# A small matmul on zeros in front of each two experts' first layers, in a ViT tower with recurrent mixing and a mixture of experts

## What is computed

```
h = patches @ W.T + b                                   # 784 tokens of 64 numbers a step
h = h + rnn(layernorm(h))                               # h_t = tanh(x_t W_ih + h_(t-1) W_hh + biases)
h = h + ffn(layernorm(h))

def ffn(x):                                             # 16 experts, 2 chosen for each token
    gate_logits = x @ gate_w + gate_b
    topk_vals, topk_idx = top_k(gate_logits, 2)
    topk_w = softmax(topk_vals)
    h = relu(einsum('bsh,ehf->bsef', x, w1) + b1)       # first layer, 64 -> 128, for all 16 experts
    expert_out = einsum('bsef,efh->bseh', h, w2) + b2   # second layer, 128 -> 64
    y = x + sum over the chosen of topk_w * expert_out
    return layernorm(y) * gamma + beta
```

## Time and profile before

| | |
|---|---|
| median of 3 runs | 514.97 us (513.32, 514.97, 515.25) |
| the profiled execution | 513.06 us, span on the core 511.0 us |
| PE busy | 493.3 us (97% of the span), 2980 matmul records |
| DVE busy | 447.3 us (88%) |
| ACT busy | 342.9 us (67%) |
| POOL busy | 183.2 us (36%) |
| mean granted clock of PE | 0.987 of full speed |

### The profile page before, as it was taken

One profiled execution on the slowest core, in us unless ns is written; L12 is line 12 of the kernel. 1 busy time (PEld: TensorE's weight loads), 2 busy tenths in 40 slices (PEclk: granted clock), 3 DMA queues, 4 the chain that ended last, 5 costly groups with the idle time before them and its releaser, 6 DMA issues.

```text
span 511.0 us, 8780 instructions
## 1 busy us (share of the span) xinstructions
PE 493.3 (97%) x2980; PEld 324.1 (63%) x2980; DVE 447.3 (88%) x881; ACT 342.9 (67%) x586; POOL 183.2 (36%) x137
## 2 busy tenths in 40 slices
PE   8789999999999999999999999999999999999993
PEld 5465666666666666666766666666666666666652
DVE  1678888989989898998989999898989899999775
ACT  1556675868677695857668586767858676665652
POOL 3220304436152443616144262515335362223133
PEclk9989999999999999999999999999999999999997
DMA  6229193957639192775819395483919366481911
GB/s 145 75 67 226 35 221 82 199 126 167 162 80 228 49 223 79 160 168 113 196 36 221 96 195 130 104 205 84 232 38 216 94 135 159 117 196 47 227 40 31
DMA packets 31067, 69.04 MB, mean 135 GB/s; under 512 B 6720, under 2 KB 10800, under 8 KB 30896
## 3 DMA queue, kind: packets, MB, share of 16 engines
q1 hardware_dynamic: 31024, 68.49, 57.9%
HBM read 60.39 MB, written 8.08 MB: 134 GB/s over the span
## 4 chain that ended last, share of the span: by engine, by line
PE 90%; DVE 2%; issue 2%; DMA 1%; ACT 1%; SPq 1%; POOL 1%; POOLq 0%; DVEq 0%; ACTq 0%
PE pZ L911 38%; PE pO L928 35%; PE pA L863 3%; PE pA L830 2%; PE pA L853 2%; PE pA L880 2%; PE pA L942 2%; DMA gbias<-gate_b 1%; PE pB L892 1%; PE pA L843 1%; PE pB L942 1%; PE pB L880 1%; PE pA L854 1%; DVE prod L679 1%; PE pO L802 0%
## 5 line engine op out<-in xcount | busy, mean ns | idle before, releaser
L503 ACT ACTIVATE hexp<-pZ,b1c 128x784 f32<-128x784 f32 x256 | 221.5, 912 | 108.9 <-PE pZ L911 108.9
L928 PE MATMUL pO<-hexp,w2s 128*64 128x392 f32 x1024 | 198.5, 503 | 0.6 <-ACT hexp L503 0.3
L911 PE MATMUL pZ<-xt,w1hi 128*128 128x392 f32 x512 | 187.8, 367 | 1.4 <-ACT xt L431 1.4
L679 DVE SCALAR_TENSOR_TENSOR prod<-pO,b2c,spread 128x392 f32<-128x392 f32 x256 | 149.8, 620 | 31.8 <-PE pO L928 30.3
L911 PE MATMUL pZ<-xt,w1lo 128*128 128x392 f32 x512 | 173.8, 340 | 0.0
L911 PEld LDWEIGHTS pZ<-xt,w1hi 128*128 128x128 f32 x512 | 96.1, 188 | 46.9 <-issue 18.3
L366 POOL TENSOR_TENSOR inv_std<-var,nhalf 112x7 f32<-112x7 f32 x48 | 82.5, 1727 | 105.3 <-DVE var L569 105.3
L928 PEld LDWEIGHTS pO<-hexp,w2s 128*64 128x64 f32 x1024 | 70.2, 136 | 75.3 <-issue 62.2
L695 DVE TENSOR_TENSOR acc<-acc,prod 128x784 f32<-128x784 f32 x111 | 111.3, 1002 | 0.1
L911 PEld LDWEIGHTS pZ<-xt,w1lo 128*128 128x128 f32 x512 | 96.4, 188 | 0.0
L379 POOL TENSOR_TENSOR h2b<-h2c,bet 112x448 f32<-112x448 f32 x15 | 18.4, 1226 | 162.3 <-DMA h2c<-h_dram 162.3
(11 more groups left out here) (114 smaller groups left out, 503.3 us busy)
## 6 DMA issues: line engine op xcount, KB each, us to landing
spread<-gates_dram SPq DMA_DIRECT2D x126, 392.0 KB, 8.9
h_dram<-h SPq DMA_DIRECT2D x16, 248.1 KB, 2.4
h2c<-h_dram SPq DMA_DIRECT2D x16, 248.1 KB, 9.0
out<-yo SPq DMA_DIRECT2D x15, 196.0 KB, 9.1
xcur<-x_in SPq DMA_DIRECT2D x16, 112.0 KB, 7.8
xcur<-x_in SPq DMA_DIRECT2D x16, 84.0 KB, 8.9
w1f<-w SPq DMA_DIRECT2D x2, 512.0 KB, 5.8
spread<-gates_dram SPq DMA_DIRECT2D x4, 196.0 KB, 3.6
```

What stands on the lines that cost most here:

```text
L503: nc.scalar.activation(hexp[u % RING][:, :].rearrange("p (b c) -> p b c", b=2), halves(pZ[u % 2]), ACT.Relu, bias=b1c[:, u:u + 1]).then_in ...
L679: nc.vector.scalar_tensor_tensor(out=prod[q % RING][:, b * HALF:(b + 1) * HALF], in0=halves(pO)[:, b, :], scalar=b2c[:, q:q + 1], in1=spre ...
L911: last = nc.tensor.matmul(halves(pZ[e % 2])[:, b, :], w[:, e, :], xt[par][:, b * HALF:(b + 1) * HALF], start=(k == 0), stop=(k == 1))
L928: last = nc.tensor.matmul(halves(pO)[k * D:(k + 1) * D, b, :], w2s[:, e, :], hexp[e % RING][:, b * HALF:(b + 1) * HALF], start=True, stop= ...
```

## The change

In front of the first of two experts' first layers (even e), once PE has waited for what `pZ` needs, PE multiplies 32 columns of zeros by a 128 x 128 block of zeros into the first 32 columns of `pZ[0]`. The matmul with `w1hi` that follows starts a new sum there and writes over them. The very first expert (n = 0) has none, so there are 16 * 8 - 1 = 127 of these.

```diff
--- before.py
+++ after.py
@@ -906,6 +906,9 @@
                     pe.wait_ge(h1_kept, 2 * 2 + 2)
                 if not known(n, 2):
                     pe.wait_ge(h_ready, n - 1)
+                if e % 2 == 0 and not known(n, 1):
+
+                    nc.tensor.matmul(pZ[0][:, 0:32], busy[:, 0:128], busy[:, 0:32], start=True, stop=True)
                 for b in range(2):
                     for k, w in enumerate((w1hi, w1lo)):
                         last = nc.tensor.matmul(halves(pZ[e % 2])[:, b, :], w[:, e, :],
```

## The result

| | before | changed |
|---|---|---|
| median | 515.04 us (513.32 to 515.25, 4 executions) | 527.90 us (526.56 to 528.64, 4 executions) |
| the profiled execution | 513.06 us, span 511.0 | 527.29 us, span 525.2 |

The changed kernel is slower: the ratio is 1.0254, with a 95% interval from 1.0222 to 1.0287, so 13.1 us (11.4 to 14.8) at 515. The forecast was 527.5 us in a range from 524.3 to 532.4.

A forecast was written before the change was run, and what follows sets the result against it. The prediction took PE to be the bound, never held by another engine through some 460 us. 124 unhidden inserts x 0.108 us = 13.4 us, added to the mean of 514.15, gave 527.5 us, range 524.3 to 532.4.

The forecast's parts named there:

- PE is the only bound: In the loop from 38 to 500 us: PE is never held by another engine, its waits adding up to 1.2 us.
- The price is a second bare load: Behind each insert: the small matmul is too short to cover the load of `w1hi`, which costs 0.108 us.
- rows 10: Profile rows of lines 952 and 956: 14 loads of 112 with 64-column matmuls start in 1.37 us, 0.098 us each.
- low side: Lower bound, from line 880's transposes: 0.093 us for each of 121 inserts, 11.3 us, on the lowest execution: 524.3.
- Three inserts of the first step are hidden, up to three more later: Experts 2, 4 and 6, ahead of waits of 1.1 and 0.6 us, cost nothing; other short waits may swallow three more.
- The forecast's base: Whole kernel before the change: 514.15 us, the mean of four executions, to which 13.4 us was added.
- PE empties ahead of the insert since it needs the full array after tiles: Behind tiles: the emptying of about 0.08 us moves from `w1hi` to the insert, at no cost of its own.
- the first rival: Behind second layers: the insert's load is pulled ahead, 98 places cost nothing, 29 still 0.108 us: 517.3 us; 5%.
- the faster one: Behind tiles: the loads of insert and `w1hi` are both taken ahead, 98 places win 0.093 us each: 508.2 us; 4%.
- A second emptying: Between the small matmul and `w1hi`: PE empties again, some 0.08 us more for each insert, 537.5 us; 4%.
- hidden behind other engines' padding: Throughout PE's list: waits that the records don't show pad PE's busy time and the inserts fill those, 514 us; 2%.

## Why the prediction was right

**PE is the only bound.** Held. PE stays at 32.00 of 32.00 us, DVE and ACT lost share, and a step grew by 0.90 us, where the eight distances of 0.11 that were added in PEld come to 0.88.

**The price is a second bare load.** Held, by four independent edits: columns (232 cost next to nothing, 392 cost 0.178), place, number and width of weights. The forecast's 0.108 us was 0.004 too low; the step gives 0.112. Read to the nanosecond, the starts of the loads put the added distance at 0.109 us behind tiles and 0.112 behind the full-array transposes, 0.110 in the mean of the eight places; the other 2 ns stay open. The prediction's own rows 10 were nearest: 0.098 us for 112 columns of weights is 0.112 for 128. Its low side was not a price of loads: the 0.093 us of line 880's transposes (0.096 from load to load) goes with the columns that pass, 112 there and 128 at 0.109 us for line 942, though the former load 128 columns and the latter 112.

**Three inserts of the first step are hidden, up to three more later.** The waits shrank by 0.1 and 0.2 us as forecast. In the last part some five inserts' worth, 0.6 us, was swallowed rather than up to three. 13.4 us was forecast, and the inserts' share of the span's 14.2 us is 0.5 + 10.8 + 2.0 = 13.3 us: the price a little low and the swallowed part a little low cancel, which is luck. The remaining 0.9 us comes from the place of the low clock at the start. The forecast's base, 514.15 us, was likewise 0.9 us below the measured median of before, and its addition 0.3 us above the measured 13.1.

**PE empties ahead of the insert since it needs the full array after tiles.** The prediction gave this cause without rows that could separate it from the change of type. The run with half the array first spoke against it, and the two in plain f32 restored it, with the addition on f32r. The price of the insert doesn't hang on it.

**The rivals.** Behind tiles the load of zeros was not pulled ahead in any f32r run; the 0.61 us ahead of it stood. That settles the first rival and the faster one, which needed the same. It did go ahead once, in plain f32 with 64 columns, where shape and type were those of the second layers. So the pull-ahead that the Trainium skill describes ("TensorE: Matmul & The Clock Gate", section "Step-by-step: what each phase is for") is there, and a change of shape stops it. The Trainium skill, "TensorEngine Tiling (Array Packing)", section "Key Properties", says that switching the tiling mode needs a drain. The runs agree: from the last second-layer load to that of `w1hi` it takes 0.75 us (246.00 to 246.75 in the earlier trace rows), two passings of 0.33 and 0.09 of emptying. A second emptying (537.5 us) didn't occur, and nothing was hidden behind other engines' padding.

The Trainium skill's floor of about 25 ns for a small matmul ("TensorE: Matmul & The Clock Gate", section "Back-to-back issue gap"), taken as the price of an insert, would have given 3.1 us. The runs show four times that, because each matmul brings a load of its own width.

## What to carry to other kernels

In f32r and in plain f32, a matmul that was too short to cover a weight load cost that load: 0.11 us for 128 columns of weights, whether 32 or 232 columns pass, 0.08 for 96 behind tiles and 0.06 for 64. The transposes are another case: there the columns that pass set the distance. Read the price of a small matmul on a full PE from the distances between load starts, not from its record or its columns. Keep matmuls of one array shape together: each entry from 64 columns into the full array cost an emptying of some 0.09 us and a bare load of 0.11, and filler on the full array neither hid nor shortened either. Filler in the tiles' own shape hid only at the one place where the two halves of the array were out of step.

## What the runs showed of the hardware that I had not expected

- An f32r matmul with 64 columns of weights behaves in the change of shapes as a full-array one: PE empties ahead of it behind 64-column matmuls in plain f32 (0.61 us idle), and not between it and a 128-column one. Its load is still priced by its own width (0.05 to 0.06 us).
- A matmul in plain f32 of 32 columns comes as two records with a load each, 0.11 us apiece at 128 columns.
- In this kernel's start, a wait of PE of 1.1 us was followed by half the clock (0.50) in one execution and by the full clock in another, where it fell only behind a later wait of 1.3 us. Where the low stretch lies moves some 0.9 us between executions of kernels that are alike there.
